# An edge convolution with a segment maximum: filling and running maximum as scans over six tiles

## The reference, cut to what is computed

```python
h = maximum(layernorm(x), 0)                 # x: 12500 x 64
x_i, x_j = h[dst], h[src]                    # 400000 edges, sorted by dst
feat = concatenate([x_i, x_j - x_i], -1)
m = maximum(feat @ W1 + b1, 0) @ W2 + b2     # W1: 128 x 64, W2: 64 x 64
out = segment_max(m, dst, 12500)             # an empty segment gives 0
return x + where(isneginf(out), 0, out)
```

## Time and profile before

| | |
|---|---|
| median of 3 runs | 4081.74 us (4079.1 to 4085.41) |
| the profiled execution | 4073.29 us, its span 4071.5 us |
| busy: TensorE, VectorE, ScalarE, GpSimd | 71%, 59%, 21%, 75% of the span |
| instructions: VectorE, ScalarE, GpSimd | 7589, 3260, 3189 |
| mean DMA rate | 109 GB/s |

### The profile page before, as it was taken

One profiled execution on the slowest core, in us unless ns is written; L12 is line 12 of the kernel. 1 busy time (PEld: TensorE's weight loads), 2 busy tenths in 40 slices (PEclk: granted clock), 3 DMA queues, 4 the chain that ended last, 5 costly groups with the idle time before them and its releaser, 6 DMA issues.

```text
span 4071.5 us, 47102 instructions
## 1 busy us (share of the span) xinstructions
PE 2888.8 (71%) x14651; PEld 1613.3 (40%) x14651; DVE 2410.9 (59%) x7589; ACT 850.4 (21%) x3260; POOL 3053.3 (75%) x3189
## 2 busy tenths in 40 slices
PE   3200099999878887878887877787887877887820
PEld 2100055555444444444444444444444444444410
DVE  5110188888666666666666666666666666666631
ACT  4420032222112212112112112112112112112100
POOL 5777777777777777777777777777777777777767
PEclk8555599999999999999999999999999999999955
DMA  9993133333333333333333333333333333333331
GB/s 372 378 414 147 37 101 105 107 107 104 82 85 85 82 85 86 81 86 86 81 85 85 84 83 85 82 85 86 81 85 85 82 84 86 81 85 85 85 85 47
DMA packets 198940, 443.48 MB, mean 109 GB/s; under 512 B 61989, under 2 KB 66658, under 8 KB 187946
## 3 DMA queue, kind: packets, MB, share of 16 engines
q1 hardware_dynamic: 54890, 219.23, 16.3%
q0 software_dynamic: 103312, 109.12, 12.9%
q10 hardware_dynamic: 40487, 112.13, 7.4%
HBM read 222.67 MB, written 217.71 MB: 108 GB/s over the span
## 4 chain that ended last, share of the span: by engine, by line
POOL 63%; issue 20%; PE 12%; DVE 2%; DMA 1%; ACT 1%; ACTq 0%; POOLq 0%; DVEq 0%; SPq 0%
POOL rows L382 58%; PE ps_g L680 10%; POOL a_edges L405 2%; POOL a_rows L438 2%; PE ps_m L699 2%; PE ps_t L690 1%; DMA blocks<-in_dst_dram,blk_idx 1%; ACT zt L456 0%; ACT shared L483 0%; DMA b_table<-shared 0%; DVE state L915 0%; PE ps_m L641 0%; DVE shared L784 0%; DVE stat L788 0%; DVE stat L782 0%
## 5 line engine op out<-in xcount | busy, mean ns | idle before, releaser
L382 POOL DMA_INDIRECT rows<-b_table,src_idx x2868 | 2740.7, 956 | 874.1 <-issue 873.2
L680 PE MATMUL ps_g<-shared,dst_all 128*128 128x512 bf16 x9509 | 2216.6, 389 | 84.7 <-DVE dst_all L944 84.4
L680 PEld LDWEIGHTS ps_g<-shared,dst_all 128*128 128x128 bf16 x9509 | 936.4, 101 | 1178.5 <-DVE dst_all L944 110.7
L887 DVE SCALAR_TENSOR_TENSOR a_fill<-a_fill,keep 128x64 f32<-128x64 f32 x3125 | 875.3, 280 | 173.9 <-DMA a_fill<-a_edges 154.6
L915 DVE SCALAR_TENSOR_TENSOR state<-state,keep,ps_m 128x64 f32<-128x64 f32 x3125 | 862.5, 276 | 83.7 <-PE ps_m L699 64.4
L901 DVE TENSOR_TENSOR rows<-rows,a_fill 128x512 f32<-128x512 f32 (+1 forms) x521 | 270.5, 560 | 1022.8 <-DMA rows<-b_table,src_idx 1022.5
L699 PE MATMUL ps_m<-w_diag,zt 128*128 128x128 f32 x3126 | 496.2, 318 | 498.1 <-ACT zt L565 494.2
L699 PEld LDWEIGHTS ps_m<-w_diag,zt 128*128 128x128 f32 x3126 | 446.4, 223 | 609.0 <-ACT zt L565 597.4
L543 ACT ACTIVATE dst_all<-ident_h,key_octet 128x128 f16<-128x128 f16 x257 | 102.7, 400 | 2421.5 <-DVE state L915 2421.1
L553 ACT ACTIVATE dst_all<-ps_g,dst_all 128x64 f32<-128x64 f32 x2056 | 450.0, 344 | 0.0
L690 PE MATMUL ps_t<-ident,rows 128*128 128x128 f32 x1563 | 216.1, 275 | 230.3 <-DVE rows L901 230.3
(11 more groups left out here) (116 smaller groups left out, 446.6 us busy)
## 6 DMA issues: line engine op xcount, KB each, us to landing
a_edges<-rows SPq DMA_DIRECT2D x80, 1250.0 KB, 14.8
a_fill<-a_edges SPq DMA_DIRECT2D x260, 384.0 KB
states<-state ACTq DMA_DIRECT2D x260, 384.0 KB, 2.4
rows<-b_table,src_idx POOLq DMA_INDIRECT x2868, 2.4
a_fill<-b_table ACTq DMA_DIRECT2D x12, 256.0 KB, 8.9
shared<-in_x_dram SPq DMA_DIRECT2D x5, 560.0 KB
b_table<-shared ACTq DMA_DIRECT2D x5, 560.0 KB
a_table<-a_rows ACTq DMA_DIRECT2D x1, 2800.0 KB
```

Of the source, the lines that this page charges most:

```text
L382: nc.gpsimd.indirect_dma_start(out=rows[:, c % RING, t * C:(t + 1) * C], out_offset=None, in_=b_table, in_offset=at(src_idx[:, q % SRC_RIN ...
L680: last = nc.tensor.matmul(ps_g[:, half, :], key_is[:, half, g, :], table[:, g, t, :], start=(g, t) == (0, 0), stop=g == PAGES - 1)
L887: nc.vector.scalar_tensor_tensor(here, before, flag(c, 0, t), here, ALU.mult, ALU.add).then_inc(fill_step, 1)
```

## The change

VectorE's 12 fill steps and 12 maximum steps of a chunk become, for each of two groups of six tiles, a head (the first tile of the group, joined to the last tile before it) and a scan over the group's 384 numbers. A scan runs along the columns of a lane: its running value is limited by a flag (minimum) and joined with the next number (maximum). For that the six tiles of a channel have to lie side by side, channel outermost, and each number needs its own flag. ScalarE writes the flags (spread_flags), turns the loaded A rows into this layout (turn_fill) and turns the states back before their store. TensorE writes the messages to PSUM in this layout, and VectorE's add reads A from it at a step of six numbers. The fill now takes a maximum instead of a sum, so the table is cleared to the lowest number instead of zero. Groups are 6 and 6 tiles instead of 8 and 4, the ring has 17 buffers with 13 ahead of the scatter, and the new buffers share room with two that are used up before the loop.

```diff
--- before.py
+++ after.py
-    RING = 18
+    RING = 17
-    GROUP = 8
+    WORK_RING = 4
+    GROUP = 6
-    PREFIX = 14
+    PREFIX = 13
...
+        def by_tile(columns, g, n):
+            return columns[:, g * GROUP * C:(g * GROUP + n) * C].rearrange("p (c t) -> p t c", t=n)
+        def steps_below(c):
+            return 2 * GROUPS * c
@@ sync @@
-                if c >= 1:
-                    sp.wait_ge(fill_step, (c - 1) * CHUNK + 1)
+                if c == 1:
+                    sp.wait_ge(fill_step, 1)
+                if c >= 2:
+                    sp.wait_ge(fill_turned, c - 1)
@@ scalar: flags, two new passes, step @@
-                nc.scalar.activation(keep[:, q % 2, 0, 0:tiles], now, ACT.Relu)
+                heads = keep[:, q % 2, 0, 0:tiles:GROUP]
+                nc.scalar.activation(keep[:, q % 2, 0, 0:tiles], now, ACT.Copy, scale=FLT_MAX)
...
+                nc.scalar.activation(heads, ones[:, 0:-(-tiles // GROUP)], ACT.Copy, scale=-FLT_MAX).then_inc(keep_ready, 1)
+            def spread_flags(c, tiles):
...
+                for g, n in groups(tiles):
+                    last = nc.scalar.activation(
+                        flag_rows[:, c % WORK_RING, g * GROUP * C:(g * GROUP + n) * C].rearrange("p (c t) -> p c t", t=n),
+                        flags_of[:, g * GROUP:g * GROUP + n].rearrange("p (c t) -> p c t", c=1).to_broadcast((P, C, n)),
+                        ACT.Copy)
+                last.then_inc(flags_spread, 1)
+            def turn_fill(c, tiles):
+                act.wait_ge(a_loaded[c % AE_RING], (c // AE_RING + 1) * 16)
+                if c >= 2:
+                    act.wait_ge(z_ready, (c - 1) * GROUPS)
+                    act.wait_ge(fill_step, steps_below(c - 1) + 1)
+                for g, n in groups(tiles):
+                    last = nc.scalar.activation(
+                        by_tile(fill_cols[:, c % 2, :], g, n),
+                        a_fill[:, c % AE_RING, g * GROUP * C:(g * GROUP + n) * C].rearrange("p (t c) -> p t c", c=C),
+                        ACT.Copy)
+                last.then_inc(fill_turned, 1)
...
-                act.wait_ge(max_step, c * CHUNK + tiles + 1)
+                if c + 3 <= CHUNKS:
+                    spread_flags(c + 3, tiles_of(c + 3))
+                    turn_fill(c + 3, tiles_of(c + 3))
+                act.wait_ge(max_step, steps_below(c) + 2 * len(groups(tiles)) + 1)
+                if c >= 2:
+                    act.wait_ge(state_stored[k % 2], c // 2 * 16)
+                for g, n in groups(tiles):
+                    last = nc.scalar.activation(
+                        state[:, k % 2, g * GROUP * C:(g * GROUP + n) * C].rearrange("p (t c) -> p t c", c=C),
+                        by_tile(state_cols[:, c % 2, :], g, n), ACT.Copy)
+                last.then_inc(state_turned, 1)
+                act.wait_ge(state_turned, c + 1)
                 act.dma_start(state_lanes[:, c * W:c * W + tiles * C], state[:, k % 2, 0:tiles * C]
                               ).then_inc(state_stored[k % 2], 16)
@@ tensor: step @@
-                        last = nc.tensor.matmul(ps_m[:, g, a * C:(a + m) * C], zt[0:m * C, g, a * C:a * C + P],
+                        here = ps_m[:, g, 0:n * C].rearrange("p (c t) -> p t c", t=n)[:, a:a + m, :]
+                        last = nc.tensor.matmul(here, zt[0:m * C, g, a * C:a * C + P],
                                                 w2_pair[0:m * C, 0:m * C], start=True, stop=True)
@@ vector @@
-            nc.vector.memset(zero_rows, 0.0).then_inc(zero_row_set, 1)
+            nc.vector.memset(zero_rows, -FLT_MAX).then_inc(zero_row_set, 1)
...
+            def fill_head(c, g, n):
...
+                nc.vector.scalar_tensor_tensor(here, before, flag(c, 1, g * GROUP), here,
+                                               ALU.min, ALU.max).then_inc(fill_step, 1)
+            def fill_scan(c, g, n):
+                part = slice(g * GROUP * C, (g * GROUP + n) * C)
+                dve.wait_ge(fill_step, steps_below(c) + 2 * g + 1)
+                nc.vector.tensor_tensor_scan(fill_cols[:, c % 2, part], flag_rows[:, c % WORK_RING, part],
+                                             fill_cols[:, c % 2, part], -FLT_MAX, ALU.min, ALU.max).then_inc(fill_step, 1)
...
-                    nc.vector.tensor_tensor(rows[:, c % RING, part], rows[:, c % RING, part],
-                                            a_fill[:, c % AE_RING, part], ALU.add).then_inc(z_ready, 1)
+                    here = rows[:, c % RING, part].rearrange("p (t c) -> p t c", c=C)
+                    nc.vector.tensor_tensor(here, here, by_tile(fill_cols[:, c % 2, :], g, n), ALU.add).then_inc(z_ready, 1)
...
+            def max_scan(c, g, n):
+                part = slice(g * GROUP * C, (g * GROUP + n) * C)
+                dve.wait_ge(max_step, steps_below(c) + 2 * g + 2)
+                nc.vector.tensor_tensor_scan(state_cols[:, c % 2, part], flag_rows[:, c % WORK_RING, part],
+                                             ps_m[:, g, 0:n * C], -FLT_MAX, ALU.min, ALU.max).then_inc(max_step, 1)
...
-                for t in range(CHUNK + LEAD):
-                    if t == CHUNK - 2 and picks_in(c + CHOOSE_AHEAD):
-                        choose(c + CHOOSE_AHEAD)
-                    if t < filled:
-                        fill(c + 2, t)
-                    if t >= LEAD:
-                        maximum(c, t - LEAD)
+                for g, n in groups(CHUNK):
+                    if g in filled:
+                        fill_head(c + 2, g, filled[g])
+                    max_head(c, g, n)
+                    if g in filled:
+                        fill_scan(c + 2, g, filled[g])
+                    max_scan(c, g, n)
+                if picks_in(c + CHOOSE_AHEAD):
+                    choose(c + CHOOSE_AHEAD)
```

More of the change, by code:

```diff
@@ L600, in _ @@
                     spread_keys(c + KEYS_AHEAD)
+            for c in range(3):
+                spread_flags(c, CHUNK)
+                turn_fill(c, CHUNK)
             for c in range(CHUNKS):
@@ L871, in flag, with last_row @@
                 return keep[:, q % 2, kind, j * CHUNK + t:j * CHUNK + t + 1]
+            def last_row(columns):
+                return by_tile(columns, GROUPS - 1, GROUP)[:, GROUP - 1, :]
             def fill_ready(c):
[L874 to L881, removed]
-                else:
[L883 to L888, removed]
+                dve.wait_ge(flags_spread, c + 1)
+                dve.wait_ge(fill_turned, c + 1)
+            def fill_head(c, g, n):
+                here = by_tile(fill_cols[:, c % 2, :], g, n)[:, 0, :]
+                if c == 0 and g == 0:
+                    before = a_fill[:, AE_RING - 1, W - C:W]
+                elif g == 0:
+                    before = last_row(fill_cols[:, 1 - c % 2, :])
+                else:
+                    before = by_tile(fill_cols[:, c % 2, :], g - 1, GROUP)[:, GROUP - 1, :]
+                if c + g > 0:
+                    dve.wait_ge(fill_step, steps_below(c) + 2 * g)
+                nc.vector.scalar_tensor_tensor(here, before, flag(c, 1, g * GROUP), here,
[5 more added lines that the diff above has]
+                                             fill_cols[:, c % 2, part], -FLT_MAX, ALU.min, ALU.max).then_inc(fill_step, 1)
             def add(c):
-                dve.wait_ge(fill_step, c * CHUNK + tiles_of(c))
+                dve.wait_ge(fill_step, steps_below(c) + 2 * len(groups(tiles_of(c))))
                 if c < CHUNKS:
@@ L959, in _ @@
                     match_keys(c)
-            LEAD = 2
             def fill_all(c):
                 fill_ready(c)
-                for t in range(CHUNK):
-                    fill(c, t)
+                for g, n in groups(CHUNK):
+                    fill_head(c, g, n)
+                    fill_scan(c, g, n)
             for s in range(ZQ):
                 dve.wait_ge(zeros_stored[s], 16 * ZEROS // ZQ)
-            nc.vector.memset(state[:, 1, W - C:W], -FLT_MAX).then_inc(carry_set, 1)
+            nc.vector.memset(last_row(state_cols[:, 1, :]), -FLT_MAX).then_inc(carry_set, 1)
             dve.wait_ge(ends_gathered, 16)
@@ L985, in _ @@
                 if c >= 2:
[L986 to L996 removed]
+                    dve.wait_ge(state_turned, c - 1)
+                for g, n in groups(CHUNK):
+                    if g in filled:
[6 more added lines that the diff above has]
+                    choose(c + CHOOSE_AHEAD)
+            dve.wait_ge(state_turned, CHUNKS - 1)
+            for g, n in groups(TAIL):
+                max_head(CHUNKS, g, n)
+                max_scan(CHUNKS, g, n)
             dve.wait_ge(last_turned, 1)
```

45 lines of the change are left out of this document (26 added, 19 removed).

## The result

| | before | after |
|---|---|---|
| time, us (median of 4 runs each) | 4080.42 (4077.64 to 4085.41) | 4226.7 (4222.53 to 4229.74) |
| ratio, 95% interval | | 1.0368 (1.0356 to 1.0381) |
| profiled execution: span / time, us | 4071.5 / 4073.3 | 4223.0 / 4224.85 |

The change makes the kernel 3.7% slower, 146 us, where 96 were forecast: the right direction and inside the range, but the size is half as much again.

The account below looks back on a forecast made before the run. GpSimd's gathers were taken to bound the kernel. Holds by fill scans, less the fill steps' own, gave +73 us at the gathers' pace and +23 before it, +96 in all: 4178 us, range 4112 to 4320 (chance 0.75).

Parts of the forecast that it names:

- What bounds the kernel: GpSimd's gathers set the pace, 11 x 1.259 = 13.85 us a step; savings on other engines are worth nothing.
- Part 1: VectorE's work per chunk: a scan takes 0.94 us; fill scans start 3.2 and 5.2 us after an add's start, A.
- Part 2: Fill scans, both inputs in SBUF, hold gathers 0.45 us a step (bounds 0.1 and 1.0); maximum scans hold nothing.
- the tied case: Gathers at fixed places after the add: first scan costs 0.25 us; step 0.25 if GpSimd wins the second, else 1.0.
- Part 3: VectorE's adds with strided second input: 0.55 or 0.8 us each, counted within the 0.45 us a step.
- alternative sum: With adds of 0.8 us: 0.75 us a step, 208 x 0.65 + 52 x 0.75 = +174 us in all.
- The first 52 steps: First regime, steps of 10.03 us on chunks gathered ahead: holds of 0.45 us each, +23 us.
- Parts 4 and 5: ScalarE's three new passes a chunk, 2.6 us or twice that: no loss; TensorE's strided message products: cost 0.
- Rival 2: TensorE becomes the bound through strided PSUM writes: 4840 us if products take four times as long; chance 0.04.
- Part 6: Start, one prefix chunk less: cost 0, or the excess if the table's stores ended more than 6.6 us later.
- Part 7: End, the last chunks' maxima and two state turns: -2.0 + 1.3 = -0.7 us, taken as 0.
- Rivals 1 and 3: Scans hold nothing or miss the gathers, 4060 us, chance 0.12; holds just graze, 0.1 a step, 4082, chance 0.09.

Follow-up runs that it names:

- the sixth experiment: The changed kernel with VectorE's choice of the picked row moved ahead of the heads and scans: 4276.29 us, ratio 1.0479.
- the kernel with both edits: The changed kernel with the fill scans' limits taken from PSUM and the adds reading side by side: 4064.35 us, ratio 0.9961 to the kernel before.
- the first full version: The changed kernel, computing everything, with A's rows turned into PSUM for the fill scans and filled rows turned back for side-by-side adds: 4073.92 us, ratio 0.9985.

## Why the prediction came out as it did

- **What bounds the kernel** was right: the time followed the length of the gathers, and their idle time stayed at 874 us wherever it is shown above. Profiled, 2740.7 us of gathers go with 4071.5 of span, 2890.0 with 4223.0, 2800.2 with 4134.4, 2833.6 with 4165.7, 2730.0 with 4062.5: the difference is 1331 to 1334 each time, and in the other kernels too.
- **Part 1**, the scan of 0.94 us out of one row of 405 ns: measured 0.948 and 0.928. The order behind the adds was right but late: the scans begin at A+3.82 and A+5.99 instead of A+3.2 and A+5.2, mostly because the pair of adds took 1.62 us instead of 1.1.
- **Part 2**, scans hold gathers: shown by the pair of kernels that move one operand each way. By the Trainium skill, page "SBUF — State Buffer", section Who interferes with whom, a VectorE instruction with two SBUF inputs contends with a GpSimd instruction that reads SBUF. These runs bear that out for the gathers, which read their indices there: one was held 1.2 us by two adds. The page also infers that descriptor generation is not held by a tensor_tensor. The prediction called this contradicted, which is too much: a gather both reads indices and makes descriptors, and no run tells which of the two was held. What the runs contradict is the conclusion that such instructions cost the gathers nothing. The size, 0.45 us a step for the scans, came out as taken, but partly by luck, since it was a choice between 0.25 or 1.0 in the tied case and 0.52 at random, and the tied case went otherwise: from 1100 to 3100 us the first scan catches a gather in 136 of 138 steps, typically for 0.57, not 0.25, and the second, which starts 0.17 us behind one, in 2. In the first regime the scans cost 0.13 a step, not 0.45: there the gathers fell elsewhere.
- **Part 3 is the step that failed.** The strided read was priced both ways, 0.55 and 0.8 us an add, and then counted "in the choice of 0.45", at nothing of its own. Measured: 0.854 us an add, 0.34 us a step of holds by the adds themselves, against 0.07 before. Its alternative sum, +174 with 0.75 a step, stands 24 us from the +150 that came; at the gathers' pace it gave 0.75 where 0.80 was measured, but as 0.6 by the scans and 0.15 by the adds, where 0.45 and 0.34 were measured, so part of that nearness is luck. The nearest row (L953, the one strided read of the earlier trace rows) had pointed there, and its value should have been the one taken. The kernel with the adds read side by side shows the same from the other side: 60 us less, which leaves 86, near the +96 forecast for the scans alone.
- **The first 52 steps** were taken at 52 x 0.45 = 23 us; measured 14, adds included. That is how the phases fell; at the sixth experiment's 1.34 us a step it would have been 70.
- **Parts 4 and 5**: no loss, as taken. ScalarE is busy 1915.6 us and its passes over strided columns took 0.9 us an instruction, a little past the long end of what was allowed (0.85); twelve message products take 1.60 us as before. Rival 2 is out; the kernel with both edits settles both parts at once.
- **Part 6**: a cost of 1 us in place of 0. The table's stores landed 5.9 us later and the prefix ended 1.1 us earlier than reckoned, which used up the 6.6 us of margin, and the first scatter waited 1.06 us longer than the usual 0.30.
- **Part 7**: with the start it is worth at most the 3 us by which the differences under the first point vary.
- **Rivals 1 and 3** fell with the gathers of 1.5 us inside fill scans. Rival 1's time of 4060 us is near what comes out, 4064, where both holds are taken away.

What stays open: why the table's stores landed 5.9 us later. That the change did it is not shown: across the ten traces the memset behind the last store starts anywhere from 341.8 to 349.0 us, at 343.8 in the kernel that differs from the one before in its ring alone and at 341.9 in the first full version. Open too is what part of a gather is held.

## What to carry to other kernels

Where GpSimd's gathers bound a kernel, an instruction of VectorE with both inputs in SBUF costs them time if a gather comes due while it runs, and merging many short ones into a few long ones can make that worse (0.07 us a step for the fill before, 0.45 after) even as VectorE's own busy time falls; put one input into PSUM, if that doesn't lengthen the loop that feeds the gathers' consumers. When a change makes an operand strided, price the operation from the nearest strided row of the trace and carry that length on into everything it delays or holds. A cost that depends on phase has to be reckoned in each regime of the kernel, since a held gather ends with what holds it, and the gathers can so come back to the same bad place step after step.

## What the runs showed of the hardware

- Two VectorE instructions with two SBUF inputs, one right behind the other, hold a gather as if they were one: 2.15 us at 810.96, where a free one takes 0.94. GpSimd gets no turn between them.
- Columns read or written at a step of 24 bytes in SBUF: VectorE's add of 384 takes 854 ns against 561 side by side; ScalarE's copy 917 (strided write) and 886 (strided read), where its relu from PSUM takes 475. The same turn of A's rows written into PSUM took 495 ns. TensorE's fp32 products, written to PSUM at that step, show no cost: twelve take 1.60 us as before, and the mean of one is 318 ns before and 318 in the kernel with the adds side by side, which writes at the same step (328 in the kernel after).
- A scan costs VectorE 2.1 ns a column, (948 - 140) / 384, about twice an add's (561 - 130) / 384 = 1.1, and as much with an input in PSUM (928 and 957 ns).
